# Embedding rows stored by the SyncE queue straight from the gather's tile, the wrapped rows copied inside DRAM

## What is computed

```python
# B=2048 examples, F=39 fields, D=16
e = stack([tbl_f[ids[:, f]] for f in range(39)], axis=1)        # (2048, 39, 16)
x0 = xk = e
for idx, (W, b) in enumerate(params):                           # 3 layers, 128 outputs each
    z = relu(einsum('bhd,bkd,hks->bsd', x0, xk, W) + b[None, :, None])
    if idx != 2: xk = z[:, :64]; direct.append(z[:, 64:])
    else: direct.append(z)
logit = sum(concatenate(direct, axis=1), axis=-1)               # sum over d: (2048, 256)
h = concatenate([logit, dense_ctx], axis=1)
y = relu(relu(h @ W_top1 + b_top1) @ W_top2 + b_top2) @ W_top3
```

## Time and profile before

| | |
|---|---|
| median of the runs | 2498.87 us |
| the profiled execution | 2500.31 us |
| its span | 2498.6 us |
| PE busy | 2385.2 us (95%) |
| DVE busy | 2230.4 us (89%) |
| POOL busy | 1709.7 us (68%) |
| ACT busy | 1501.2 us (60%) |
| DMA packets, rate | 267897, mean 193 GB/s |
| HBM read and written | 470.96 MB and 9.84 MB |

### The profile page before, as it was taken

One profiled execution on the slowest core, in us unless ns is written; L12 is line 12 of the kernel. 1 busy time (PEld: TensorE's weight loads), 2 busy tenths in 40 slices (PEclk: granted clock), 3 DMA queues, 4 the chain that ended last, 5 costly groups with the idle time before them and its releaser, 6 DMA issues.

```text
span 2498.6 us, 27181 instructions
## 1 busy us (share of the span) xinstructions
PE 2385.2 (95%) x7840; PEld 1468.9 (59%) x7840; DVE 2230.4 (89%) x1358; ACT 1501.2 (60%) x1798; POOL 1709.7 (68%) x1093
## 2 busy tenths in 40 slices
PE   0599999999999999999999999999999999999999
PEld 0266666666666666666666666666666666666653
DVE  0599999999999999999999999999999999999960
ACT  0366666666666666666666666666666666666652
POOL 6478777777777777677777777777776777754340
PEclk9899999999999999999999999999999999999999
DMA  2877877787777778777787877788787777867620
GB/s 69 237 207 190 222 210 199 190 214 209 190 210 209 208 182 217 208 197 199 213 216 178 215 211 202 190 215 218 181 211 212 206 182 213 222 183 202 199 62 0
DMA packets 267897, 481.11 MB, mean 193 GB/s; under 512 B 20075, under 2 KB 42715, under 8 KB 267797
## 3 DMA queue, kind: packets, MB, share of 16 engines
q1 hardware_dynamic: 146950, 275.14, 41.7%
q10 hardware_dynamic: 100480, 200.29, 28.9%
q0 software_dynamic: 20448, 5.45, 1.9%
HBM read 470.96 MB, written 9.84 MB: 192 GB/s over the span
## 4 chain that ended last, share of the span: by engine, by line
PE 70%; POOL 11%; issue 6%; DMA 6%; DVE 4%; ACT 2%; ACTq 0%; SPq 0%; POOLq 0%; DVEq 0%
PE z L796 34%; PE z L775 33%; POOL emb L409 7%; DMA emb<-in_tbl,idx 5%; DVE prod L479 4%; POOL lo_parts L251 4%; PE z L897 1%; DMA x_pairs<-x_transposed 1%; PE xk L897 1%; PE hi_copy L766 1%; ACT hi_parts L610 1%; PE direct L897 1%; DMA x_diag<-x_transposed 0%; ACT xk L630 0%; ACT xk L631 0%
## 5 line engine op out<-in xcount | busy, mean ns | idle before, releaser
L479 DVE TENSOR_TENSOR prod<-x_pairs,xk 128x2048 f32<-128x2048 f32 x640 | 1440.9, 2281 | 119.4 <-PE z L796 73.1
L775 PE MATMUL z<-prod,w_plain 128*128 128x512 f32 (+2 forms) x2688 | 1264.6, 595 | 40.2 <-DVE prod L479 40.2
L251 POOL TENSOR_TENSOR lo_parts<-prod,hi_parts 128x1024 fp32r<-128x1024 f32 x384 | 917.3, 2389 | 509.0 <-ACT hi_parts L610 486.0
L610 ACT CAST hi_parts<-prod 128x1024 fp32r<-128x1024 f32 x766 | 798.6, 1049 | 715.6 <-DVE prod L479 512.0
L796 PE MATMUL z<-hi_parts,w_lo 128*128 128x512 f32 (+1 forms) x1536 | 857.7, 558 | 1.1 <-DVE lo_parts L251 0.7
L409 POOL DMA_INDIRECT emb<-in_tbl,idx x624 | 701.9, 1125 | 196.0 <-issue 175.3
L775 PEld LDWEIGHTS z<-prod,w_plain 128*128 128x128 f32 (+2 forms) x2688 | 510.2, 190 | 440.1 <-issue 365.7
L796 PE MATMUL z<-hi_parts,w_hi 128*128 128x512 f32 (+1 forms) x1536 | 611.0, 398 | 0.0
L796 PE MATMUL z<-lo_parts,w_hi 128*128 128x512 f32 (+1 forms) x1536 | 606.7, 395 | 0.0
L796 PEld LDWEIGHTS z<-hi_parts,w_lo 128*128 128x128 f32 (+1 forms) x1536 | 289.9, 189 | 196.3 <-issue 145.0
L796 PEld LDWEIGHTS z<-lo_parts,w_hi 128*128 128x128 f32 (+1 forms) x1536 | 292.3, 190 | 189.5 <-issue 148.4
(11 more groups left out here) (69 smaller groups left out, 652.0 us busy)
## 6 DMA issues: line engine op xcount, KB each, us to landing
x_pairs<-x_transposed SPq DMA_DIRECT2D x64, 2432.0 KB, 16.2
x_pairs<-x_transposed ACTq DMA_DIRECT2D x64, 2432.0 KB, 18.6
x_diag<-x_transposed SPq DMA_DIRECT2D x128, 546.0 KB
x_diag<-x_transposed ACTq DMA_DIRECT2D x64, 546.0 KB
x_pairs<-x_transposed SPq DMA_DIRECT2D x64, 256.0 KB, 19.6
emb<-in_tbl,idx POOLq DMA_INDIRECT x624
x_diag<-x_transposed SPq DMA_DIRECT2D x128, 78.0 KB
x_transposed<-stage SPq DMA_DIRECT2D x32, 156.0 KB
```

The costliest lines, as they stand in the source:

```text
L251: engine.tensor_tensor(lo_parts[0:rows, place:place + m, :], held[0:rows, at:at + m, :], hi, ALU.subtract).then_inc(done, 1)
L479: nc.vector.tensor_tensor(prod[0:rows, pos % RING, 0:n, :], a, xk.unsqueeze(1).broadcast_to([rows, n, N]), ALU.mult).then_inc(prod_ready, 1)
L610: nc.scalar.copy(hi_parts[0:rows, place:place + m, :], held[:, at:at + m, :]).then_inc(hi_ready, 1)
L775: return nc.tensor.matmul(z[n][:], w, held[0:rows, i, :], start=first, stop=last)
```

## The change

The gathered tile `emb` is stored to `xt` as it stands, one piece of 16 values (64 bytes) for each example and field, so that a row of `xt` is now in (example, d) order instead of (chunk, half of d, d, example). The 20 wrapped rows are copied from rows 0 to 19 of `xt` to rows 39 to 58 by a DMA from DRAM to DRAM, which SP issues once the store has landed. The PE transposes, the ACT copies, the identity, `stage` and their semaphores are gone. The two reductions read (example, d) order. `ST_DMAS`, by which `xt_stored` is counted, goes from 4 to 2, and POOL's `start_group` now waits for `xt_stored` (both DMAs of the group before) instead of for the transposes. Declarations of `stage`, `ident`, `turned` and of the four semaphores, which are only taken out, are left out here.

```diff
-X0_DIAG_DMAS, X0_PAIRS_DMAS, ST_DMAS = 2 * DIAG, 3, 4
+X0_DIAG_DMAS, X0_PAIRS_DMAS, ST_DMAS = 2 * DIAG, 3, 2
...
@@ SyncE
             def store_group(bt):

                 first = ahead(bt * (P * D))
-                sp.wait_ge(stage_ready, 2 * (bt + 1))
-                cols = xt[:, bass.ds(first, P * D)].rearrange(
-                    "f (c e n) -> f c e n", c=CHUNKS, e=2)
-                for half in range(2):
-                    src = stage[half:2 * F:2].rearrange("p c d b -> p c (d b)")
-                    sp.dma_start(cols[0:F, :, half, :], src).then_inc(xt_stored, 16)
-                    sp.dma_start(cols[F:F + WRAP, :, half, :], src[0:WRAP]).then_inc(xt_stored, 16)
+                sp.wait_ge(gathered, 16 * F * (bt + 1))
+                cols = xt[:, bass.ds(first, P * D)].rearrange("f (b d) -> b f d", d=D)
+                rows = emb[:].rearrange("p (f d) -> p f d", d=D)
+                sp.dma_start(cols[:, 0:F, :], rows).then_inc(xt_stored, 16)
+
+            def store_wrap(bt):
+
+                cols = xt[:, bass.ds(ahead(bt * (P * D)), P * D)]
+                sp.wait_ge(xt_stored, 16 * (ST_DMAS * bt + 1))
+                sp.dma_start(cols[F:F + WRAP], cols[0:WRAP]).then_inc(xt_stored, 16)
...
                 sp.dma_start(x0_pairs[c % 2][:, TX - 1, :], src.partition_broadcast(P)
                              ).then_inc(x0_pairs_in[c % 2], 16)
+                if store:
+                    store_wrap(bt + 1)
...
             store_group(0)
+            store_wrap(0)
@@ GpSimd
-            nc.gpsimd.memset(ident[:], 0.0).then_inc(ident_zero, 1)
-            pool.wait_ge(ident_zero, 1)
-            nc.gpsimd.affine_select(out=ident[:], in_=ident[:], compare_op=ALU.not_equal, fill=1.0,
-                                    base=0, pattern=[[-1, P]], channel_multiplier=1
-                                    ).then_inc(ident_ready, 1)
-
...
                     pool.wait_ge(idx_in, 16 * bt)
-                    pool.wait_ge(turned_ready, 2 * bt)
+                    pool.wait_ge(xt_stored, 16 * ST_DMAS * bt)
                     pool.sem_inc(waits_held, 1)
@@ VectorE
-                                        direct01[:].rearrange("p (d b) -> p b d", b=CB),
+                                        direct01[:].rearrange("p (b d) -> p b d", d=D),
...
-                                        z[2][:].rearrange("p (d b) -> p b d", b=CB),
+                                        z[2][:].rearrange("p (b d) -> p b d", d=D),
@@ ScalarE
-            def fill_stage(bt):
...
-            fill_stage(0)
             act.wait_ge(xt_stored, 16 * ST_DMAS)
...
-                        if c == 1 and not last:
-                            fill_stage(bt + 1)
-
-                            act.wait_ge(stage_ready, 2 * (bt + 2))
                         round_splits(2, slice(EARLY[2], None), slot, pos, used_by, chunk)
@@ TensorE
-            def transpose_group(bt):
...
-                    if k == turn_at:
-                        transpose_group(turn)
...
-            pe.wait_ge(ident_ready, 1)
-            transpose_group(0)
...
-                    if c == 1 and not last:
-                        layer(2, slot, pos, lows, bt + 1, 1)
-                    else:
-                        layer(2, slot, pos, lows)
+                    layer(2, slot, pos, lows)
```

More of the change, by code:

```diff
@@ L153, in build @@
         emb = sb("emb", [P, F * D])
-        stage = sb("stage", [P, CHUNKS, D // 2, CB])
-        ident = sb("ident", [P, P])
         w_plain = [sb(f"w{n}_plain", [P, len(PLAIN_TILES[n]), S]) for n in SPLITS]
@@ L189, in build @@
         hi_copy = ctx.enter_context(nc.psum_tensor("hi_copy", [P, 2, N], F32))
-        turned = [hi_copy[:, 0, :], hi_copy[:, 1, :]]
         direct01 = ps("direct01")
@@ L206, in build @@
         top_weights_in = sem("top_weights_in")
-        ident_zero = sem("ident_zero")
-        ident_ready = sem("ident_ready")
         first_idx_in = sem("first_idx_in")
@@ L212, in build @@
         gathered = sem("gathered")
-        turned_ready = sem("turned_ready")
-        stage_ready = sem("stage_ready")
         xt_stored = sem("xt_stored")
@@ L807, in split_parts, with layer @@
                 ins.then_inc(slot_free, 1)
-            def layer(n, slot, pos, lows, turn=None, turn_at=None):
+            def layer(n, slot, pos, lows):
                 last_slot = len(FIRST_TILE) - 1
```

## The result

The changed kernel takes 2590.34 us (median of 4 runs, 2590.07 to 2592.76), against 2499.73 for the kernel before on the same chip: ratio 1.0364, 95% interval 1.0349 to 1.038. It is slower, as forecast, but by 91 us where 225 were forecast; the measured time is 10 us from that of the first rival (about 2600, the store over before the pairs loads). The profiled execution has a span of 2588.6 us.

What follows compares the result with a forecast made beforehand. PE was taken to bound the kernel. Per group 16.15 + 1.3 - 1.85 = 15.6 us, times 14 is 218.4; with + 1.9 + 5.3 that is 225.6, giving 2724 us, range 2580 to 2880.

Steps and rivals of the forecast that it cites:

- the first rival: SP's store of small pieces is over before the pairs loads, at 9.5 ns a piece: about 2600 us, chance 0.18.
- What bounds the kernel: In each group PE sets the pace, busy for 144.36 of 145.20 us; DVE has 6 us to spare.
- The gain of the removal: PE's transposes (1.09 us) and the wait ahead of them (0.76) go: 1.85 us per group, 15 times.
- Where the loss comes from: In chunk 2 POOL waits for the wrap copy behind SP's pairs loads; PE loses 16.15 us in each of 14 groups.
- The price of a small piece: On the DMA engines, a 64-byte piece of the store costs 27 ns, so the store takes 8.4 us.
- What comes, 1: The store: 4992 pieces of 64 bytes, 312 per DMA engine, 8.4 us; bounds 3.0 and 12.2 us.
- The turns: Beside ACT's pairs load the queues alternate packet by packet; 101 pieces per engine are left, and the store ends at 910.7.
- POOL's wait: At start_group in chunk 2 POOL goes on at 925.1 instead of 907.4, 17.7 us late.
- One for one from POOL to PE, less 1.55 us: Before layer 2, PE moves with POOL's gathers beyond about 1.55 us of room: 16.15 us lost per group.
- PE's clock: After each stall PE may run at 1.2 GHz again: 1.3 us per group, bounds 0 and 1.7.
- The fifteenth group: Without gathers, ACT's wait at load_last_band delays its first layer 2 cast: +1.9 us.
- The start: The first store and wrap copy land at 67.4 instead of 62.11: +5.3 us, bounds 0 and +9.

Runs made afterwards that it cites:

- the first experiment: The changed kernel, but POOL waits only for the store that reads emb, no longer for the wrap copy: 2470.4 us, ratio 0.9883 to the kernel before.
- store beside ACT's load: The changed kernel with SP's store moved behind its wait for the first product, to go out together with ACT's pairs load: 2743.2 us, ratio 1.0979.
- three stores: The changed kernel with the small-piece store made three times, two to a spare tensor ahead of the real one; the copy waits for all: 2777.7 us, ratio 1.1117.

## Why the prediction was right or wrong

**What bounds the kernel: right.** With the waits away PE is busy in all 143.0 us of a group.

**The gain of the removal: right.** 15 x 1.85 = 28 us were forecast; the first experiment gained 30 (2500.7 to 2470.4), and with the transposes put back the ratio to the kernel before went from 0.9883 to 0.9999, which is 29.

**Where the loss comes from: right.** POOL's `start_group` waits for the copy, the copy stands behind SP's pairs loads, POOL's gathers push the low parts of layer 2, and PE stops there, in 14 groups. Two experiments that each break one link, the wait or the order of the queue, take the loss away.

**The price of a small piece: wrong, and it is the step that failed.** "What comes, 1" took 27 ns from the window's store of 512-byte pieces, as the nearest row. Measured are 11.6, of which 9.6 are busy time, the measure in which the 27 were taken. The other bound, 9.5 ns a row from POOL's gathers, was near, in part by luck: that queue's 20448 packets hold 79872 rows, about four each, so a packet there costs 37 ns. A better row stood in the trace of before, the load of the indices at the start: 144 packets, 128 of them of 156 bytes, at 16.9% of 16 x 0.8 us (1.4 to 2.2 us), 15 ns each. With it the store would have been over at 897.4 of the forecast's clock, before ACT's traffic at 898.4. So 64, 156 and 512 bytes go with 9.6, 15 and 27 ns; no run changed the size alone. The error grew in the next step: at 11.6 ns the store was over in 3.7 us, before ACT's load began, and there was nothing left to take turns with. Forecast were 101 pieces per engine left over, and a store end at 910.7 instead of about 896 in the forecast's clock.

**The turns: right, but they weren't reached.** One packet of each queue in turn was assumed; 1041 against 1042 were seen when the store was put there. With a long store 2778 was measured where 2775 had been worked out with such turns. The one row of before that looked harsher, 64 packets beside 476, was the end of four short stores, and why so few went there stays open.

**POOL's wait: 9.74 us, forecast 17.7, by the first rival 10.6.** 7.1 us of the difference are the step from the forecast's store to one that is over before the loads. The last 0.9 are in the rival's own chain, which had the copy land 1.5 us behind SP's last load: it landed 1.8 ahead of it in the group shown.

**One for one from POOL to PE, less 1.55 us: near, and in part by luck.** The three kernels with a wait, each group's period less the 143.3 of the first experiment:

| kernel | POOL's wait per group | less 1.55 | period, group | cost |
|---|---|---|---|---|
| changed | 9.7 | 8.2 | 151.9 | 8.6 |
| store beside ACT's load | 21.1 | 19.5 | 162.0 | 18.8 |
| three stores | 23.0 | 21.4 | 163.9 | 20.6 |

The first row hides two errors that nearly cancel. From the store's issue to the end of POOL's low parts of layer 2 the group shown takes 52.1 us in the changed kernel (921.76 to 973.90) and 44.8 in the first experiment (878.66 to 923.44): of the 9.7 us of wait 7.4 arrive, so more than 2 are taken up on the way, where 1.25 were put in for POOL. What brings the cost back up is PE's clock.

**PE's clock: the drop came, and so did its price.** In the changed kernel, after the stall, from the busy times by window (granted clock third from last):

```profile
962.70:969.30 6.60, 6.54 (x15) 4.52 (x16) 2.29 (x1) 1.04 (x1) 6.29 (x5) 0.55 0.00 0
```

At 0.55 most of these 6.6 us ran at 1.2 GHz, after an idle time of 6.2 us. The forecast had POOL set the pace here. It doesn't: PE is busy for 6.54 of the 6.60 us and falls behind POOL. POOL's last two low parts of the chunk and PE's start on the last of them, in the changed kernel and then in the first experiment:

```profile
969.04 4.86 POOL L244 TENSOR_TENSOR lo_parts<-prod,hi_parts 128x1024 fp32r<-128x1024 f32 x2
975.97 0.40 PE L764 MATMUL z<-hi_parts,w_lo 128*128 128x512 f32 x1
```

```profile
918.57 4.87 POOL L244 TENSOR_TENSOR lo_parts<-prod,hi_parts 128x1024 fp32r<-128x1024 f32 x2
923.78 0.40 PE L764 MATMUL z<-hi_parts,w_lo 128*128 128x512 f32 x1
```

PE is 2.1 us behind POOL where it was 0.3 behind: 1.7 us for the clock, where 1.3 were put in (1.6 with the store beside ACT's load, 1.0 with three stores). 7.4 and 1.7 are 9.1, and this group is 9.0 us longer than that of the first experiment. The pages agree: the same 7712 matmuls keep PE busy for 2400.3 us against 2368.7, 2.3 per group, a part of which PE would have waited in any case.

**The fifteenth group: nothing came.** 1.9 us were put in for ACT's wait there. The profiled spans of the changed kernel and the first experiment differ by 120.5 us, and 14 groups of 8.6 are all of that.

**The start.** The first store landed within 5.2 us of its issue (54.27 to 59.49, when SP issues the copy that waits for it), and the first diag load went out at 62.8 against 62.2 before: +0.6, where 5.3 were forecast. It is the same wrong price.

**The Trainium skill's two sentences.** DMA: Bandwidth & Descriptors, Anatomy of one DMA — SWDGE (gpsimd) path (2.0 us and the bytes at 436 GB/s; the prediction names the section Bandwidth), gave an estimate of 2.7 us for the store; 5.2 were measured, so its figure is too low for 4992 pieces, though its verdict, over before ACT's load, was right. The rule in its Specifications, that transfers under 512 bytes fall below line rate, is borne out in the rate: 319 KB in 3.7 us are 86 GB/s, where ACT's load, all but alone, has 216 (0.97 MB in 4.5 us). It doesn't follow that a piece is dear: 9.6 ns of busy time are less than any larger packet read here took. The read-modify-write that the page gives as the reason is seen in no run.

**Forecast and chances.** The sum again with the measured wait: 14 x 8.6 = 120 for the wait, less the 30 of the first experiment (the start's +0.6 is in them): 2590, on the 2499.7 of before. The forecast gave the right mechanism 0.78 between two cases and weighted them 0.60 to 0.18 the wrong way round.

## What to carry to other kernels

When a buffer is handed from one reader to another, let the writer wait for the DMA that reads it, and for no later DMA that is counted on the same semaphore: here that one number was 120 us. A short DMA that others wait for belongs ahead of the bulk loads in its queue, or on its data's first path; behind them its landing time is about that of the bytes queued before it. And when the nearest row is eight times the size, look for a nearer one: a load of 156-byte pieces stood in the first 3 us of the trace. It mattered here, because the price of 9.5 ns gave a loss of 100 us and that of 27 ns one of 225, as one has the store over before the next load and the other beside it. Last, a stall costs twice: the wait, and the slow clock behind it, unless another engine really sets the pace there.

## What the runs showed that I had not expected

A write of 64 bytes from SBUF to DRAM is as cheap for a DMA engine as a gathered row of the same size (9.5 ns): 9.6 ns of busy time, 11.6 ns of pace, with 5000 of them in one DMA that took SP 0.43 us to issue. Such a store beside another queue's load is a different thing: packets of 64 bytes and of 2 KB went one for one, so 312 pieces of 64 bytes that take 3.7 us alone took 14 beside 2 KB packets (traffic from 980.3 to 994.5 us in the group shown). They held up the loads behind them, and SP itself: its issue of the pairs load took 14.1 us, against 0.6 to 0.7 in the changed kernel.

```profile
979.83 14.13 SPq L258 DMA_DIRECT2D x_pairs<-x_transposed  x1
```
